# Six attention passes over a graph: the running sums move from VectorE to TensorE and ScalarE, and block numbers are loaded one at a time

## The reference

```
e      = leaky_relu(xl[src] + xr[dst], 0.2)          # GATv2; 3125 self loops are added to the edges
logit  = einsum('ehc,hc->eh', e, att)
m      = segment_max(logit, dst)
a      = exp(logit - m[dst])
out    = segment_sum((a / segment_sum(a, dst)[dst])[:, :, None] * xl[src], dst)
# GAT: logit is a sum of one number of the source and one of the target, then leaky_relu
# transformer: logit = sum(Q[dst] * K[src]) per head, the sum is over V[src]
# GIN: agg = segment_sum(x[src], dst), without weights
```

## Time and profile before

| | us |
|---|---|
| median of three runs (7677.63 to 7682.41) | 7680.22 |
| profiled execution | 7675.66 |
| its span, first to last instruction | 7673.7 |
| TensorE busy (74%) | 5664.7 |
| VectorE busy (68%) | 5190.8 |
| ScalarE busy (40%) | 3098.6 |
| GpSimd busy (46%) | 3538.9 |

### The profile page before, as it was taken

One profiled execution on the slowest core, in us unless ns is written; L12 is line 12 of the kernel. 1 busy time (PEld: TensorE's weight loads), 2 busy tenths in 40 slices (PEclk: granted clock), 3 DMA queues, 4 the chain that ended last, 5 costly groups with the idle time before them and its releaser, 6 DMA issues. The chain is left out here.

```text
span 7673.7 us, 135823 instructions
## 1 busy us (share of the span) xinstructions
PE 5664.7 (74%) x28772; PEld 4504.7 (59%) x28773; DVE 5190.8 (68%) x17524; ACT 3098.6 (40%) x10492; POOL 3538.9 (46%) x3878
## 2 busy tenths in 40 slices
PE   2788377768888488857887968886968887747776
PEld 1566266647777266646665866665856665624455
DVE  7665388858888566658998458998369996453313
ACT  0111166636666266625553335553335553200025
POOL 0667276635555077705664006663026661047730
PEclk9999999989999588879998989998989998856678
DMA  1000211232223034436665036664056662023330
GB/s 30 3 3 3 46 49 47 47 55 75 73 73 70 29 103 102 101 92 199 177 176 144 0 121 182 175 176 103 0 168 180 176 175 59 19 84 100 101 62 17
DMA packets 336360, 689.85 MB, mean 90 GB/s; under 512 B 96524, under 2 KB 193734, under 8 KB 335814
## 3 DMA queue, kind: packets, MB, share of 16 engines
q0 software_dynamic: 209536, 581.61, 29.1%
q1 hardware_dynamic: 110592, 98.06, 4.1%
q10 hardware_dynamic: 15942, 7.24, 0.4%
HBM read 605.77 MB, written 80.89 MB: 89 GB/s over the span
## 5 line engine op out<-in xcount | busy, mean ns | idle before, releaser
L943 POOL DMA_INDIRECT arena<-tab_l,idx x2320 | 2201.8, 949 | 1028.8 <-issue 563.5
L1020 PE MATMUL bank<-arena,onehots 128*128 128x264 f32 (+3 forms) x6496 | 1978.6, 436 | 332.8 <-DVE onehots L852 179.6
L981 PE MATMUL bank<-arena,spreads 128*128 x5568 | 1457.4, 370 | 600.4 <-ACT spreads L1034 248.0
L1020 PEld LDWEIGHTS bank<-arena,onehots 128*128 128x128 f32 x6496 | 1308.4, 221 | 668.9 <-DVE onehots L852 199.7
L981 PEld LDWEIGHTS bank<-arena,spreads 128*128 128x128 f32 x5568 | 965.7, 205 | 832.7 <-issue 765.1
L1213 DVE TENSOR_TENSOR acc<-acc,bank 128x264 f32 (+3 forms) x1624 | 656.8, 404 | 495.3 <-PE bank L1020 483.7
L1034 ACT ACTIVATE spreads<-bank 128x256 f32<-128x256 f32 x1392 | 522.9, 376 | 897.4 <-PE bank L969 893.6
L1108 DVE TENSOR_TENSOR arena<-arena,bank 128x512 f32<-128x512 f32 x928 | 630.3, 681 | 265.6 <-ACT stats L1056 148.7
L861 ACT ACTIVATE onehots<-iota_row,slot_loc 128x128 f32<-128x128 f32 x1856 | 632.3, 391 | 18.6 <-PEq L1726 14.3
L943 POOL DMA_INDIRECT arena<-tab_l0b,idx x464 | 441.6, 952 | 373.0 <-ACT arena L1074 234.7
L1074 ACT ACTIVATE arena<-arena,stats 128x64 f32<-128x64 f32 (+1 forms) x1856 | 538.3, 363 | 8.8 <-PE bank L1020 3.8
(11 more groups left out here) (333 smaller groups left out, 9289.2 us busy)
## 6 DMA issues: line engine op xcount, KB each, us to landing
tab_l<-arena SPq DMA_DIRECT2D x150, 384.0 KB, 3.1
arena<-tab_l,idx POOLq DMA_INDIRECT x2320, 3.6
arena<-tab_l0a,idx POOLq DMA_INDIRECT x464, 2.5
arena<-tab_l0b,idx POOLq DMA_INDIRECT x464, 2.7
rec_dram<-arena POOLq DMA_INDIRECT x417, 2.1
tab_l<-arena SPq DMA_DIRECT2D x25, 132.0 KB, 1.8
tab_l0b<-arena SPq DMA_DIRECT2D x25, 128.0 KB, 1.7
residual<-X SPq DMA_DIRECT2D x1, 3200.0 KB
```

What stands on the lines that cost most here:

```text
L943: pool.indirect_dma_start(out=rows_sb[:, a, t, 0:width], out_offset=None, in_=table[:, :], in_offset=bass.IndirectOffsetOnAxis(ap=idx[:, a ...
L981: mm = pe.matmul(z[x.k % 2][:, t, 0:cw], spreads[:, x.k % 2, t * P:t * P + P], qtab[:, block_no[w % BG], 0:cw], start=True, stop=not gatv2)
L1020: mm = pe.matmul(sums[x.k % 2], onehots[:, x.a, GT * x.k + t, :], rhs, start=t == 0, stop=t == GT - 1)
```

## The change

**The sums.** TensorE adds a third product to the two of "add_up": the identity by the block's rows of `acc`. ScalarE copies the result back to `acc`. VectorE no longer adds, it only scales the block's rows once per batch. On TensorE "add_up" now stands ahead of "target" in the slot.

**The spread matrix.** The slots' node numbers are written to DRAM once as 16-bit numbers (`loc_dram`). In each pass SP's queue reads them back in halves of a batch, the same 1024 numbers to all 128 partitions (`loc_ring`). VectorE compares them with the partition's number, 512 columns at a time for two groups, which gives the transposed one-hot matrices (`spread_ring`). Transposes and ScalarE's copies go. The one-hot matrices are made four slots later, and VectorE makes both of a group in one operation.

**GATv2.** leaky_relu(z) is 0.2 z + 0.8 max(z, 0). The first part is linear, so that its product with `att` is worked out for the nodes, as two further columns of both tables (rows of 130 and 258 numbers). ScalarE copies these two columns of the sum, VectorE does max(z, 0) times 0.8 att in one operation and sums in another.

**Block numbers.** `block_at` loads one number, at each product and each copy that needs it.

```diff
-            LAG = dict(one_hots=0, turn=1, target=2, logit=3, weigh=14, add_up=15, keep=16)
+            LAG = dict(spread=0, one_hots=4, target=2, logit=3, weigh=14, add_up=15, keep=16)
...
-            def next_blocks(engine, shifted_by, col):
+            def block_at(engine, i, w, lag):
                 return nc.values_load_multi_w_load_instructions(
-                    block_of[0:1, shifted_by, ds(col, BG)], engines=[engine], min_val=0, max_val=NT - 1,
+                    block_of[0:1, ds(G16 + G16 * i + w - lag, 1)], engines=[engine], min_val=0, max_val=NT - 1,
...
+                @block.sync
+                def _(sp):
+                    def batch_fn(s, a, use):
+                        for h in range(2):
+                            if needed(4 * s + 2 * h - 2):
+                                sp.wait_ge(S["spread_made"].sem, S["spread_made"].at(4 * s + 2 * h - 2))
+                                sp.sem_inc(tick.sem, 1)
+                            sp.dma_start(loc_ring[:, h, :],
+                                         loc_dram[0:1, ds(BT * P * s + h * HALF, HALF)].to_broadcast([P, HALF]))\
+                              .then_inc(loc_in[h].sem, 16)
...
                 @block.tensor
-                        x = Group(i, w, LAG["turn"])
-                            pe.transpose(pot[x.k % 2][:, 0:P], onehots[:, x.a, GT * x.k, :], ident[:, :])
-                            pe.transpose(pot[x.k % 2][:, P:2 * P], onehots[:, x.a, GT * x.k + 1, :], ident[:, :])\
-                              .then_inc(S["oh_turned"].sem, 1)
+                        x = Group(i, w, LAG["add_up"])
+                        if x.there:
...
+                            for t in range(GT):
+                                rhs = rows_sb[:, x.a, GT * x.k + t, 0:wc] if gin else weighted[:, x.k % 2, t, 0:wc]
+                                mm = pe.matmul(sums[x.k % 2], onehots[:, x.a, GT * x.k + t, :], rhs,
+                                               start=t == 0, stop=gin and t == GT - 1)
+                            if not gin:
+                                sum_block = block_at(mybir.EngineType.PE, i, w, LAG["add_up"])
+                                if needed(x.g):
+                                    pe.wait_ge(S["added_up"].sem, S["added_up"].at(x.g))
+                                if x.k == 0:
+                                    pe.wait_ge(S["rescaled"].sem, S["rescaled"].at(x.batch + 1))
+                                mm = pe.matmul(sums[x.k % 2], ident[:, :], acc[:, sum_block, 0:wc],
+                                               start=False, stop=True)
+                            mm.then_inc(S["summed"].sem, 1)
                         x = Group(i, w, LAG["target"])
                         if x.there and not gin:
-                            pe.wait_ge(S["spread_made"].sem, S["spread_made"].at(x.g + 1))
+                            target_block = block_at(mybir.EngineType.PE, i, w, LAG["target"])
...
                 @block.scalar
-                        x = Group(i, w, LAG["turn"])
+                        x = Group(i, w, LAG["keep"])
                         if x.there:
-                            act.activation(spreads[:, x.k % 2, :], pot[x.k % 2], ACT.Copy)\
-                               .then_inc(S["spread_made"].sem, 1)
+                            keep_block = block_at(mybir.EngineType.Activation, i, w, LAG["keep"])
+                            act.wait_ge(S["summed"].sem, S["summed"].at(x.g + 1))
+                            act.activation(acc[:, keep_block, 0:wc], sums[x.k % 2], ACT.Copy)\
+                               .then_inc(S["added_up"].sem, 1)
                         x = Group(i, w, LAG["target"])
                         if x.there and gatv2:
                             act.wait_ge(S["target_spread"].sem, S["target_spread"].at(x.g + 1))
-                            act.activation(rows_sb[:, x.a, GT * x.k:GT * x.k + GT, D:D + cw], z[x.k % 2][:, :, 0:cw],
-                                           ACT.Copy, scale=0.2)\
-                               .then_inc(S["activated"].sem, 1)
+                            act.activation(raw[:, x.a, 2 * BT:4 * BT].rearrange("p (t h) -> p t h", h=2)
+                                           [:, GT * x.k:GT * x.k + GT, :], z[x.k % 2][:, :, width:width + 2],
+                                           ACT.Copy).then_inc(S["activated"].sem, 1)
...
                 @block.vector
+                            dve.tensor_scalar(spread_ring[:, quad % 2, :],
+                                              loc_ring[:, h, quad % 2 * 4 * P:quad % 2 * 4 * P + 4 * P],
+                                              small[:, 0:1], None, ALU.is_equal).then_inc(S["spread_made"].sem, 1)
...
-                            dve.tensor_tensor(pr, pr, src[:, :, D:D + cw], ALU.max).then_inc(S["leaked"].sem, 1)
+                            dve.scalar_tensor_tensor(pr, pr, 0.0, att[:, 0:width].unsqueeze(1)
+                                                     .to_broadcast([P, GT, width]), ALU.max, ALU.mult)\
+                               .then_inc(S["multiplied_rows"].sem, 1)
...
-                            dve.tensor_tensor(av, av, sums[x.k % 2], ALU.add).then_inc(S["added_up"].sem, 1)
```

More of the change, by code:

```diff
@@ L720, in _ @@
                           .then_inc(multiplied.sem, 1)
-            loaded.base += 16 * 7
+                        pe.transpose(PS[1][0:q4, q * P:q * P + P], slots[:, q * q4:(q + 1) * q4, 3], ident[:, :])\
+                          .then_inc(multiplied.sem, 1)
+            loaded.base += 16 * 11
             step.base += 5
-            placed.base += 2
-            multiplied.base += 4
+            placed.base += 3
+            multiplied.base += 8
         def find_borders():
@@ L980, in slot_fn @@
                             for t in range(GT):
-                                mm = pe.matmul(z[x.k % 2][:, t, 0:cw], spreads[:, x.k % 2, t * P:t * P + P],
-                                               qtab[:, block_no[w % BG], 0:cw], start=True, stop=not gatv2)
+                                column = (GT * x.k + t) % 4 * P
+                                mm = pe.matmul(z[x.k % 2][:, t, 0:cw], spread_ring[:, x.k // 2 % 2, column:column + P],
+                                               targets[:, target_block, 0:cw], start=True, stop=not gatv2)
                                 if gatv2:
@@ L1272, in edge_pass @@
                 S["mid"].base += NB * 9
+                S["spread_made"].base += NB * 4
+                for h in range(2):
+                    loc_in[h].base += 16 * NB
             if gatv2:
-                per_group += ("activated", "leaked")
+                per_group += ("activated", "multiplied_rows")
             if hgt:
@@ L1465, in multiply @@
                                 pe.wait_ge(D_["dve_out"].sem, D_["dve_out"].at(dve_ops * (j - 1)))
+                        if lin is not None:
+                            for k in range(kb):
+                                pe.matmul(lins[a], xT[:, a, k * P:k * P + P], lin[:, k, :], start=k == 0,
+                                          stop=k == kb - 1)
                         for k in range(kb):
@@ L1935, in transformer_layer @@
             project(lambda j: hbuf[:, j, :], 2, wo, 256,
[L1936 removed]
+                    dve_out=lambda dve, j, a, ps, lin: dve.tensor_tensor(X[:, j, :], X[:, j, :], ps, ALU.add)
                     .then_inc(D_["dve_out"].sem, 1), bias=vecs[:, 0:D])
@@ L1972, in layer_3 @@
                  (cols[:, 16:24], A["L3_gnn_beta"].rearrange("(m p) -> p m", p=P)))
-            hid = [arena[:, NP * m:NP * m + NP] for m in range(7)] + [border[:, 0:NP]]
+            hid = [arena[:, NP * m:NP * m + NP] for m in range(8)]
             turned = [PS[0][:, 0:D], PS[7][:, 0:D]]
```

204 lines of the change are left out of this document (115 added, 89 removed).

## The result

The changed kernel takes 8930.8 us (median of four runs, 8910.5 to 8934.5), the kernel before 7681.3 us in the runs beside it: 1.162 times as long, 95% interval 1.160 to 1.164. The forecast was 10,950 us, range 9600 to 11,900. The loss is 1250 us where 3270 were forecast. The sign held, and so did one of the two mechanisms, the loop in GATv2; the other and larger term of the sum, the stop of TensorE at every block load, did not.

A forecast was written before the change was run, and what follows sets the result against it. VectorE was taken to pace the transformer and second GATv2 passes, GpSimd the last; after the change TensorE would. Six passes +3249 us and 30 outside, on 7676, gave 10,955, forecast as 10,950 us, range 9600 to 11,900.

The forecast's parts named there:

- the loop in GATv2: GATv2 passes: TensorE's slot and ScalarE's weighing follow one another; second layer 6.6 us a slot against 3.4, first 4.9 against 2.7.
- the stop of TensorE at every block load: Two block loads a slot on TensorE, each a stop of 0.67 us, 1.34 a slot.
- I take 0.67, the row as it stands: Price of one single-number block load on TensorE, read off the old transformer pass: 0.67 us, the load itself 0.59.
- nothing covers it: the products queued ahead are through: Ground for the 0.67 us: in the old transformer pass TensorE had no queued products left to run during the load.
- the fixed price: TensorE's block load costs the same for one number as for eight: load 0.59 us, stop 0.67.
- the price per number: TensorE's block load costs in proportion to its numbers: one costs 74 ns and the stop shrinks to 0.15 us.
- The cheap-load rival: Single-number loads at 74 ns, each stop 0.52 us shorter, over 1440 slots 1500 us: total 9450; chance 0.12.
- The clock: TensorE's granted clock: 0.60 first GATv2, 0.75 second, 0.75 GAT, 0.88 transformer; mixed slots 6.0, 7.7, 4.4, 4.45 us.
- Terms per batch: Waits once per eight slots: transformer and GAT 4.3 us, 0.54 a slot; GATv2 0.26 a slot for ScalarE's exponential.
- The last pass and what lies outside: Last pass stays at 620 us, paced by GpSimd's gathers; work outside the passes, such as slope operations, adds 30 us.
- Of what would show it: Profile signs: 2784 TensorE loads near 0.59 us, 0.7 us gaps, two GATv2 waits, clock under 0.8, transformer VectorE under 65%.
- the other two: Further signs of being wrong: single loads well under 0.3 us, or the second GATv2 pass under 1300 us.

The follow-up runs named there:

- the order kernel: Changed kernel with TensorE's sums and third product moved back behind its target products and small products, all loads kept: 7657.5 us, ratio 0.9965 to the kernel before.

## Why the prediction was right in sign and wrong in size

**The loop in GATv2: right.** Its members, its place and the two waits named for it are in the profile (L1068 for L1030, 1678 us; L1005 for L1109, 381 us in the second pass alone), and opening it in two different places gives back 1111 and 592 us of the two passes. Its terms in us, forecast and measured, in the slot of 2900.35: sums and load 1.56, 0.96; third product and load 1.12, 0.55; target products and hop 2.02, 2.04; small copy 0.20, 0.07; weighing 1.17, 1.18; denominators and hop 0.27, 0.47.

**"I take 0.67, the row as it stands": the step that failed.** It stood on "nothing covers it: the products queued ahead are through", which held for a load behind two transposes. In the new order the first load stands behind the sums (0.89 us) and the second behind the third product too, and I carried the price over without asking how much is queued ahead of each. At full clock the step put 1.34 us into each of 240 slots of six passes, 1930 us. With a fifth of the loads on TensorE and an eighth on ScalarE only 198 us came back; with the stops that this kernel has of its own, some 14 us a pass, I estimate under 300 us for what the single loads cost in all. A transformer slot of 2.2 us between waits shows nothing of them. The smaller part is the duration: 0.30, where both the fixed price (0.59) and the price per number (0.074) were off. The Trainium skill (DMA: Bandwidth & Descriptors, Latency and other measured facts) puts a floor of about 600 ns under tensor_load; the loads of eight agree (0.59), the single ones lie at half of it, and the measurement decides. The cheap-load rival (9450, by way of a price of 74 ns) was the nearest, but by another mechanism: the load costs little because it is covered.

**The clock: half right.** Forecast 0.60, 0.75, 0.75, 0.88; measured 0.63, 0.92, 0.83, 0.95. With no stops at the loads the products lie closer together, and I take it that the clock follows. In the second GATv2 pass this is 264 of the 473 us of my miss (7.7 less 6.6 us a slot, 240 slots); the other 206 are the loop (6.6 less 5.74). In the first GATv2 pass the clock did fall as forecast. There the loads do count: with eight at once the clock is 0.77 and the pass 137 us shorter, with eight from an even place 0.82 and 204 us, against 0.63 (0.65 in the kernel with loads written twice). But with the order moved back and all single loads kept it is 0.94, so it goes with the gaps and not with the loads as such. That shorter gaps keep the clock up was not isolated.

**Terms per batch: right, somewhat too small.** Forecast 4.3 us a batch in the transformer pass: 2.5 for the denominators, 1.0 small products, 0.8 for the rescale. Measured in the batch shown 2.79, 1.1 (L992, L1036, L1041, L1052) and 1.15; the 0.79 behind L1290 and the 0.43 without a releaser were missing. Since these waits are all that is left there, the transformer pass comes to 3.2 us a slot, not 4.45, and VectorE is 81% busy, not under 65%.

**The last pass and what lies outside: right** (623 for 620, 20 us for 30). The slot numbers' broadcast loads cost nothing that shows.

**Of what would show it:** 2784 loads are there, but of 0.30; the 0.7 us between the products are not there; the two GATv2 waits are. The clock is under 0.8 in the first GATv2 pass (0.63), not in the second (0.92); VectorE is busier than 65% in the transformer; the last pass is as said. A transformer pass under 800 us was named as the sign that I am wrong, and it came (762); the other two did not (single loads of 0.30 us, second GATv2 pass 1377).

**Open:** why a transformer pass of the order kernel takes 716 us and not less, when VectorE has 614, TensorE 604 and GpSimd 457 us of work in it, and why the three transformer passes of the kernel in which VectorE adds differ (768, 791, 721) though they have the same work.

## What to carry to other kernels

Before moving a block within one engine's order, write down what its first wait needs and what stands behind it on that engine, and follow that through the other engines back to the start: a loop over two engines turns parallel work into a sum, here 1111 us in two passes for one block moved. Look for a second loop behind the first; here there was one. A load into registers is to be priced by what is queued ahead of it on its engine, not by the stop it once caused elsewhere; in these runs it was bare right behind a wait that had just ended, behind very short work, and where two stood in a row. And moving an operation to another engine paid only in the stages where the engine it left was the one that the others waited for: decide it for each stage.

## What the runs showed of the hardware

- A register load of one number took 0.30 us on TensorE's queue, 0.28 on ScalarE's, 0.31 on VectorE's; of eight numbers 0.59 and 0.55 when they started at a multiple of eight. The same eight, started one or six numbers behind a multiple, took 1.94 us on TensorE. Such starts were tried on TensorE only.
- TensorE's queue ran 1.8 us ahead of its products (a load of 0.59 us at 4909.9 that stands ahead of the sums of 4911.74), and that load left no gap. Two in a row, 1.4 us behind 0.87 us of products, left one of 0.9 us.
- In the first GATv2 pass, with the same products, the mean granted clock was 0.63 and 0.65 (two profiles) with the single loads and the loop, 0.82 with loads of eight from an even place, 0.94 with the single loads and the loop opened by TensorE's order.
